# Moving the second half of the MoE router one round later in a loop over token tiles

## The reference, cut to what matters

```
def _layernorm(x, g, b):
    mu = jnp.mean(x, axis=-1, keepdims=True)
    var = jnp.var(x, axis=-1, keepdims=True)
    return (x - mu) * jax.lax.rsqrt(var + LN_EPS) * g + b
...
x = x + _layernorm(attention(_layernorm(x)))          # 16 heads, causal, ALiBi
u = _layernorm(x)
z = _layernorm(u, ln_g, ln_b)
probs = jax.nn.softmax(z @ rW + rb, axis=-1)          # 8 experts
topv, topi = jax.lax.top_k(probs, 2)
mask = jnp.sum(jax.nn.one_hot(topi, E) * topv[..., None], axis=-2)
w = mask / jnp.maximum(jnp.sum(mask, axis=-1, keepdims=True), 1e-8)
hid = gelu(z @ W1[e] + b1[e])                         # for every expert e
mixed = sum over e of w[e] * (hid @ W2[e] + b2[e])
x = x + _layernorm(u + mixed)
```

## Time and profile before

| what | us |
|---|---|
| median of 2 runs | 3254.18 (3254.07 to 3254.28) |
| the profiled execution | 3249.44 |
| its span on the slowest core, core 1 | 3247.9 |
| spans of the eight cores | 3228.3 to 3247.9 |
| mean granted TensorE clock of the cores | 0.834 to 0.838 |

### The profile page before, as it was taken

How to read it: one execution, slowest core, us unless ns; L and a number is a source line. 1 busy time by engine, 2 the same in 40 slices (tenths; PEclk the granted TensorE clock), 3 DMA queues, 4 the chain that set the end, 5 groups by cost and what they waited for, 6 DMA issues and landing times.

```text
span 3247.9 us, 40212 instructions; the slowest of 8 cores (3228.3 to 3247.9 us)
## 1 busy us (share of the span) xinstructions
PE 2784.6 (86%) x11536; PEld 1412.9 (44%) x18304; DVE 965.3 (30%) x1845; ACT 986.8 (30%) x1989; POOL 64.9 (2%) x78
## 2 busy tenths in 40 slices
PE   1768888988888744489999999999599999999996
PEld 1435554222222222245555555554245555555553
DVE  4456333555555556410110111013110110011004
ACT  0001656666666456412112111211202111211221
POOL 0000000000000000000000000000000000000000
PEclk9988555555555676699999999999799999999998
DMA  5132000000000343444346434643736434533542
GB/s 131 27 39 27 2 1 1 1 1 1 1 1 1 63 144 111 96 92 78 60 71 104 78 52 78 98 69 94 154 53 104 78 53 78 97 65 58 93 78 91
DMA packets 92894, 205.07 MB, mean 63 GB/s; under 512 B 4248, under 2 KB 12568, under 8 KB 92704
## 3 DMA queue, kind: packets, MB, share of 16 engines
q0 software_dynamic: 75952, 142.64, 27.6%
q1 hardware_dynamic: 16752, 59.85, 6.0%
HBM read 319.96 MB, written 25.17 MB: 106 GB/s over the span
## 4 chain that ended last, share of the span: by engine, by line
PE 78%; DVE 7%; DMA 6%; issue 3%; ACT 3%; DVEq 3%; ACTq 1%; SPq 0%
PE pb L947 27%; PE pb L981 25%; PE pb L473 11%; PE pb L439 9%; PE pb L328 3%; DVE recf_s L501 2%; PE pb L376 2%; DMA x1r<-xuscr 1%; DMA y<-outb 1%; DMA x0t<-x 1%; ACT slabs L447 1%; PE pb L523 1%; DVE outb L909 1%; DVEq L360 1%; DVE st L600 1%
## 5 line engine op out<-in xcount | busy, mean ns | idle before, releaser
L947 PE MATMUL pb<-Trz,fsl 128*128 128x512 bf16 x4096 | 904.1, 383 | 3.1 <-DVE accB L995 3.1
L981 PE MATMUL pb<-fsl,hidT 128*128 128x512 bf16 x4096 | 894.1, 381 | 11.3 <-DVE accB L995 8.2
L955 ACT ACTIVATE hidT<-pb,b_s 128x512 bf16<-128x512 f32 x512 | 324.0, 684 | 1385.6 <-PE pb L947 1383.1
L447 ACT ACTIVATE slabs<-pb,alibi_s 128x512 bf16<-128x512 f32 (+2 forms) x896 | 450.4, 553 | 508.4 <-PE pb L439 508.4
L947 PEld LDWEIGHTS pb<-Trz,fsl 128*128 128x128 bf16 x4096 | 396.8, 97 | 165.1 <-issue 7.9
L981 PEld LDWEIGHTS pb<-fsl,hidT 128*128 128x128 bf16 x4096 | 396.4, 97 | 163.0 <-issue 3.6
L473 PE MATMUL pb<-slabs,vgD 128*65 128x512 bf16 (+2 forms) x836 | 348.7, 512 | 54.6 <-DVE slabs L455 54.4
L992 DVE SCALAR_TENSOR_TENSOR accA<-pb,wS,accA 128x512 f32<-128x512 f32 x64 | 48.1, 751 | 1097.1 <-PE pb L981 1096.8
L439 PE MATMUL pb<-qT,kT 64*128 64x512 bf16 (+2 forms) x896 | 320.0, 472 | 50.5 <-ACT slabs L447 38.8
L940 PEld LDWEIGHTS <-fsl 128*128 128x128 bf16 x2048 | 202.3, 99 | 255.8 <-issue 20.5
L974 PEld LDWEIGHTS <-hidT 128*128 128x128 bf16 x2048 | 201.2, 98 | 257.4 <-issue 18.4
(11 more groups left out here) (108 smaller groups left out, 1187.6 us busy)
## 6 DMA issues: line engine op xcount, KB each, us to landing
fsl<-W POOLq DMA_DIRECT2D x64, 2048.0 KB, 15.5
xpp<-x SPq DMA_DIRECT2D x8, 1024.0 KB, 5.8
x0t<-x SPq DMA_DIRECT2D x16, 512.0 KB, 4.0
xuscr<-x1t SPq DMA_DIRECT2D x16, 512.0 KB, 3.3
xuscr<-ut SPq DMA_DIRECT2D x16, 512.0 KB, 3.3
x1r<-xuscr SPq DMA_DIRECT2D x8, 1024.0 KB, 6.5
y<-outb SPq DMA_DIRECT2D x8, 1024.0 KB, 4.6
accA<-xuscr SPq DMA_DIRECT2D x8, 512.0 KB, 3.9
```

The costliest lines, as they stand in the source:

```text
L447: e.activation(slab, sb[:, 0:qw], AF.Exp, bias=bias, scale=0.125),
L947: tw=tw: e.matmul(b[:, 0:tw], lw, rhs, start=(cc == 0), stop=(cc == CCH - 1)),
L955: e.activation(dst, b[:, 0:tw], AF.Gelu, bias=b1_s[:, e_ * FCH + fc: e_ * FCH + fc + 1], scale=1.0),
L981: e.matmul(b[:, 0:512], lw, rhs, start=(fc == 0), stop=(fc == FCH - 1)),
```

## The change

`rt2`, with the lines that set up its views, is taken out of `p3_B23` and becomes a function of its own, `p3_B3`. The loop calls `p3_B3(i - 7)` as the first thing of round i, ahead of `p3_B23(i - 6)`, and runs one round more (TC + 8 instead of TC + 7). The line that defined `ub` was not used. The body of `rt2` is the same.

```
-            ub = u_t[:, (tc % 4) * 1024:(tc % 4) * 1024 + 1024]
+
+        def p3_B3(tc):
+            par = tc % 2
+            lg = lgS[:, par * 64: par * 64 + 64]
             wv = wS[:, tc * E:(tc + 1) * E]
             wb = wbf_t[:, (tc % 16) * 8:(tc % 16) * 8 + 8]
...
         a_re_d = {}
-        for i in range(TC + 7):
+        for i in range(TC + 8):
+            if 0 <= i - 7 < TC:
+                p3_B3(i - 7)
             if 0 <= i - 6 < TC:
                 p3_B23(i - 6)
```

## The result

The changed kernel takes 3208.55 us (median), the kernel before 3255.79 in the same runs; the ratio is 0.9855 (95% interval 0.9841 to 0.9868), 47 us or 1.45% less. Forecast were 3209.7 us, a gain of 44.5. These medians count one slow execution of each kernel, while the ratio goes by the fast ones alone, whose medians are 3208.54 and 3254.28, 45.7 us apart. The profiled execution took 3204.4 us; its slowest core is core 3, not core 1.

What follows compares the result with a forecast made beforehand. A ring of waits between DVE and ACT was taken to bound the loop. Start 8.54 + ten rounds 10 x (13.97 - 10.87) + tail 4.95 = 44.5 us; 3254.18 - 44.5 = 3209.7 us, range 3203 to 3222.

Steps and rivals of the forecast that it cites:

- The ring: Loop before the change: Exp, router, statistics and x1 on DVE, two ACT normalisations, next Exp; 13.88 us a round.
- the 48.3 us of waits: All 16 waits of DVE's router block for the routing Exp in the kernel before; upper limit of any gain.
- DVE as the next bound: Loop after the change: DVE's own work per round, router block included, sets the pace at 10.87 us.
- The gain of the start: Loop's first rounds: statistics of tile 5 begin when its copies end, 8.54 us earlier.
- The tail: From the statistics of tile 15 to the FFN's start: 34.3 us instead of 39.25, gain 4.95.
- ACT with a margin of 0.4 us: ACT in the loop's new rhythm: Exp waits longer for the maximum, but ACT's round still fits by 0.4 us.
- item 4: ACT's timetable from DVE's round start: second normalisation at 9.12, Exp at 14.4, first normalisation done at 19.5, next due 19.9.
- rival (a): SP's queue of three chained 512 KB transfers a round becomes the loop's bound; at 12.0 us a round 3218 us; chance 0.12.
- The threshold of 10.95: Period in us a round of SP's chained transfers from which that queue, not DVE, decides the FFN's start.
- (b): The loop's wait moves to ACT: round 11.9 us, 3220 us, or no gain, 3254; chance 0.06, of which 0.02 no gain.
- (c): SP's queue runs at its pace beside the weight loads, 21.5 us a round: slower than before, 3294 us; chance 0.02.
- the prediction's estimate from it: SP's three chained transfers each 1.8 us longer from HBM latency at high load: 15.8 us a round, gain under 6 us.

Runs made afterwards that it cites:

- e9: Kernel before with two more small ACT operations in each tile's third normalisation; copies of tile 5 to first FFN matmul 197.1 to 197.6 us, before 188.8 to 189.4.
- e11: Kernel before with four more small DVE operations in each tile's router block; copies of tile 5 to first FFN matmul 201.3 to 201.9 us, no ratio.
- e10: Changed kernel with two more small ACT operations in each third normalisation; copies of tile 5 to first FFN matmul 145.3 to 145.8 us on six cores, 147.5 and 149.4 on two.
- e8: Changed kernel with maximum, Exp and router batched for all 16 tiles behind the loop, and SP's three streams on separate semaphores; ratio to the kernel before 0.9797.
- e1: Changed kernel with SP's three streams in the loop on semaphores of their own, so transfers chain only within a stream; ratio to the kernel before 0.9829.
- e5: Changed kernel with the router block in 8 DVE operations instead of 12, SP's single chain kept; ratio to the kernel before 0.9855.
- e7: Changed kernel with maximum, Exp and router done once for all 16 tiles behind the loop, SP's single chain kept; ratio to the kernel before 0.9856.
- e6: Changed kernel with the router block in 8 DVE operations instead of 12 and SP's three streams on separate semaphores; ratio to the kernel before 0.9813.

## Why the prediction was right

*The ring (13.88 us) and the 48.3 us of waits.* Right; e9 and e11 lengthen two different members of it, and both show in full in the length of the round (14.42 and 14.80 us against 13.88) and in B. On core 1 the waits of line 768 for Exp, sixteen of 48.3 us before, are now three:

```profile
  ACT lgS L755: 1.8, 3
```

*DVE as the next bound, 10.87 us a round.* Right on six cores. On core 1 the statistics of tile 5 begin at 1152.45 and those of tile 15 at 1261.39:

```profile
1152.45 0.69 DVE L600 BATCH_NORM_STATS2 st<-x1t 128x6 f32<-128x512 f32 x1 [0.78 <-ACT x1t L660]
```

```profile
1261.39 0.69 DVE L600 BATCH_NORM_STATS2 st<-x1t 128x6 f32<-128x512 f32 x1
```

That is 108.94 us, 10.89 a round. The gain of the start was to be 8.54: from the copies of tile 5 (1151.06) to their statistics it is 1.39 us, before 1169.88 - 1159.95 = 9.93, so 8.54. The tail was to be 34.3 us: the FFN begins at 1295.48, so 34.09.

```profile
1295.48 4.86 PE L952 MATMUL pb<-Trz,fsl 128*128 128x512 bf16 x13
```

The sum, 44.5, is B's change from 188.9 to 144.4 on core 1. The FFN itself begins 8.8 us before the 1304.3 of the forecast there: the copies of tile 5 came at 1151.06 and no longer at 1159.95, since this execution reached the loop 3.6 us earlier and its first rounds took 5.3 less. The forecast had nothing for either. Over the eight cores A moved by 1.6 us in the mean.

*ACT with a margin of 0.4 us and a longer wait of Exp.* Too tight a figure, without consequence: e10 puts 0.54 us more on ACT in every round and the rounds stay. By e8 ACT's work is 9.4 us a round without the Exp of a tile (0.19), so about 9.6 in the changed kernel and not 9.9 (item 4's 19.5 less 9.12, less the wait of Exp), and the margin was 0.3 us wider than I had it.

*SP's chain, rival (a), chance 0.12.* The mechanism was right and it does decide, but on two cores only. I took 10.4 us a round from one core and two rounds; the eight cores of the changed kernel have 9.8 to 11.15. The threshold of 10.95 was counted from the 21.3 us between the copies of tile 5 and the chained issue at 1181.21 on core 1 of the kernel before. On core 2 these are 23.7 us in the changed kernel (1158.52 to 1182.23), which brings the threshold down to 10.6, and so its 10.94 a round made it 4 us late. For core 3 the rival's formula gives 1270.11 + 1.3 + 34.3 = 1305.7 for the FFN's start; it is 1306.95. Core 3's B is 4.4 us longer than core 1's, and core 3 is the slowest of the profiled execution, so that both cases are in its time. The step that was missing is that the time is that of the slowest of eight cores, while the sum was made for one.

*That the execution still came out as forecast* (3204.4 against 3204.9) is in part luck: core 3 lost 4.4 us in the loop against the forecast and its FFN is 3.2 us shorter than that of core 1 before (1895.9 and 1899.1 us from the first FFN matmul to the end), a difference between cores that every kernel here shows. On core 1, for which the sum was made, the span fell by 56.3 us, the 44.5 and 11.8 more from the earlier start and a shorter FFN. The mean of the eight spans fell by 45.7, of which 43.4 are B.

*Rivals (b) and (c).* ACT's or TensorE's wait did not take the stall's place in the rounds. The pace of the earlier trace rows did not come back: 11.15 us is the most, with 29% more traffic on core 1 (156 GB/s against 121). The Trainium skill, "DMA: Bandwidth & Descriptors", section "Latency and other measured facts", gives 2 us of HBM latency at high load, and the prediction's estimate from it, 1.8 us more for each transfer, was 15.8 us a round. No core of the changed kernel comes near it, and in e1, where the three transfers go out together and core 3 moves up to 395 GB/s in a slice (last section), the loop is as fast as DVE allows. So the trace speaks against the estimate. It does not say how much of a transfer's 3 to 4 us is such a latency, nor that the load here was high in the page's sense.

What stays open: why the chain is slower on cores 2 and 3 in this execution, on cores 6 and 7 in e10 and on cores 0 and 1 in e5 (11.07 and 11.28 us a round, the others 10.0 to 10.3). The late cores are neighbours each time, but no trace here shows what they have in common, and no run was made on it.

## What to carry to other kernels

When an in-order engine waits for a short operation of another in-order engine, follow the ring round once and add it up; moving the waiting block one round later takes out the wait and every other engine's part of the ring, but the block's own length stays, so the gain is the ring less the largest sum of one engine. Before the gain is booked, put every serial resource of a round beside that sum, a DMA queue with chained transfers included, and for each core: of two that stand within a few per cent of each other, shortening one may bring nothing to the slowest core. Here a shorter DVE alone left the time where it was (e5 and e7), and became worth 11 and 13 us of B once SP's streams were apart (e6 and e8). To see such things, compare a stretch between two marks on each core rather than the time of the slowest.

## What the runs showed of the hardware that I had not expected

Three 512 KB transfers of one queue that wait for one another take 9.8 to 11.15 us a round depending on the core, in the same execution of the same program. Issued together, two of them take longer on core 3 (x0t 5.6 us in the median to landing instead of 4.1, the ut store 4.2 instead of 3.3) and the x1t store less (2.7 instead of 3.5), and all three are done well within a round. The view of the DMAs from 1160 to 1250 in e1 on that core (rate in 40 slices; stream, count, size, median us to landing), and after it that of the changed kernel from 1160 to 1270:

```profile
GB/s 202 197 284 271 291 4 0 342 257 100 0 22 395 286 7 4 60 382 240 16 0 144 340 215 0 0 228 304 178 4 0 279 266 155 0 0 362 220 120 0
...
x0t<-x SPq DMA_DIRECT2D x9, 512.0 KB, 5.6
xuscr<-x1t SPq DMA_DIRECT2D x8, 512.0 KB, 2.7
xuscr<-ut SPq DMA_DIRECT2D x8, 512.0 KB, 4.2
```

```profile
x0t<-x SPq DMA_DIRECT2D x10, 512.0 KB, 4.1
xuscr<-x1t SPq DMA_DIRECT2D x10, 512.0 KB, 3.5
xuscr<-ut SPq DMA_DIRECT2D x9, 512.0 KB, 3.3
```

DVE shows small gaps of 0.3 to 0.4 us that no semaphore explains, in four of ten rounds on core 1 (11.01 to 11.13 us, the others 10.77 or 10.78), and likewise in the kernel before (14.11 to 14.23 among rounds of 13.88); they are the 0.1 us a round that the forecast carried over from there.
